# Attention scores of float32 queries and keys: one float32 matmul against three float32r passes over split operands

## What is computed

```python
q = apply_rope(rmsnorm(q, q_norm_w), rope_cos, rope_sin)
k = apply_rope(rmsnorm(k, k_norm_w), rope_cos, rope_sin)
scores = jnp.einsum('bhtd,bhsd->bhts', q, k) * scale
scores = LOGIT_SOFTCAP * jnp.tanh(scores / LOGIT_SOFTCAP)
scores = jnp.where(mask[None, None], -jnp.inf, scores)
attn = jax.nn.softmax(scores, axis=-1)
out = jnp.einsum('bhts,bhsd->bhtd', attn, v)
```

## Time and profile before

| | |
|---|---|
| median of 3 executions | 1161.46 us |
| lowest to highest | 1160.77 to 1165.43 us |
| the profiled execution | 1160.57 us |
| its span, first to last instruction | 1158.8 us |
| PE busy | 1036.8 us, 89% |
| DVE / ACT / POOL busy | 613.2 / 493.5 / 416.7 us |
| mean granted PE clock | 0.977 of full speed |

### The profile page before, as it was taken

How to read it: one execution, slowest core, us unless ns; L and a number is a source line. 1 busy time by engine, 2 the same in 40 slices (tenths; PEclk the granted TensorE clock), 3 DMA queues, 4 the chain that set the end, 5 groups by cost and what they waited for, 6 DMA issues and landing times.

```text
span 1158.8 us, 18069 instructions
## 1 busy us (share of the span) xinstructions
PE 1036.8 (89%) x5813; PEld 859.1 (74%) x5813; DVE 613.2 (53%) x1429; ACT 493.5 (43%) x905; POOL 416.7 (36%) x601
## 2 busy tenths in 40 slices
PE   4999999999999999999999999996879887777774
PEld 4689898899989889988888899895545554444443
DVE  3674546566586567578565856853374211111116
ACT  1355555455545455554544565454220222333320
POOL 2232224432225643222763322374026143444440
PEclk9999999999999999999999999998899999999995
DMA  9960000001001100100110000002010598889866
GB/s 364 340 210 0 0 0 1 1 1 38 1 1 53 71 18 1 37 1 1 68 43 8 19 19 1 1 19 83 10 55 5 134 233 211 224 224 234 227 131 217
DMA packets 59189, 95.74 MB, mean 83 GB/s; under 512 B 8203, under 2 KB 41750, under 8 KB 58608
## 3 DMA queue, kind: packets, MB, share of 16 engines
q1 hardware_dynamic: 46880, 80.66, 21.7%
q0 software_dynamic: 12240, 14.16, 6.4%
HBM read 62.17 MB, written 42.15 MB: 90 GB/s over the span
## 4 chain that ended last, share of the span: by engine, by line
PE 72%; DMA 12%; DVE 9%; issue 3%; POOL 1%; ACT 1%; SPq 0%; DVEq 0%; POOLq 0%; ACTq 0%
PE ps L1145 21%; PE ps L1168 11%; PE ps L1192 11%; DMA wds<-in_wd 9%; PE ps L1181 9%; PE ps L1357 4%; PE ps L1229 3%; PE ps L1372 3%; PE ps L1154 2%; PE ps L1175 2%; PE ps L1157 2%; DVE arena L866 2%; PE ps L1304 2%; DMA acc<-wos,arena 1%; PE ps L1126 1%
## 5 line engine op out<-in xcount | busy, mean ns | idle before, releaser
L392 POOL TENSOR_TENSOR holdp<-neghalf 128x1 f32<-128x1 f32 x139 | 30.1, 216 | 508.7 <-DVE ss L760 267.8
L541 ACT ACTIVATE prob<-ps,rn 128x512 f32<-128x512 f32 (+3 forms) x256 | 121.1, 526 | 178.4 <-PE ps L1168 178.3
L1145 PE MATMUL ps<-wh,hth 128*128 128x384 f32 x512 | 177.8, 347 | 8.5 <-DVE wl L714 4.6
L760 DVE TENSOR_REDUCE ss<-arena 128x8 f32<-128x1024 f32 x64 | 78.1, 1220 | 198.4 <-ACT arena L525 198.3
L1145 PE MATMUL ps<-wh,htl 128*128 128x384 f32 x512 | 172.4, 337 | 0.0
L1145 PE MATMUL ps<-wl,hth 128*128 128x384 f32 x512 | 172.3, 337 | 0.0
L1168 PE MATMUL ps<-qt,kt 128*128 128x512 f32 (+3 forms) x512 | 149.6, 435 | 11.6 <-DVE arena L779 5.8
L525 ACT ACTIVATE arena<-ps 128x1024 f32<-128x1024 f32 x64 | 65.6, 1025 | 221.4 <-PE ps L1145 221.4
L1192 PEld LDWEIGHTS ps<-vx,prob 128*128 128x128 f32 x1280 | 152.9, 191 | 4.0 <-POOL prob L439 0.8
L1192 PE MATMUL ps<-vx,prob 128*128 128x129 f32 (+1 forms) x1280 | 153.4, 274 | 0.5 <-POOL prob L439 0.5
L504 POOL DMA_INDIRECT acc<-wos,arena x64 | 90.2, 1409 | 142.4 <-ACT wos L649 105.0
(11 more groups left out here) (165 smaller groups left out, 1605.1 us busy)
## 6 DMA issues: line engine op xcount, KB each, us to landing
wgus<-in_wgu SPq DMA_DIRECT2D x64, 352.0 KB
wds<-in_wd SPq DMA_DIRECT2D x64, 176.0 KB
slot_rows<-pay SPq DMA_DIRECT2D x1, 7728.0 KB, 35.5
arena<-slot_rows SPq DMA_DIRECT2D x64, 120.8 KB, 3.3
warena<-in_wqkv SPq DMA_DIRECT2D x1, 4992.0 KB, 20.2
acc<-zrow SPq DMA_DIRECT2D x2, 2048.0 KB, 30.1
warena<-acc SPq DMA_DIRECT2D x8, 512.0 KB, 7.5
wos<-in_wo SPq DMA_DIRECT2D x1, 2048.0 KB, 28.3
```

The source lines that it names most:

```text
L541: act_(prob[:, OFF[j]:OFF[j] + w], sflat[:, OFF[j]:OFF[j] + w], ACT.Tanh, scale=rn[:, bass.ds(head(n), 1), TT + j:TT + j + 1].squeeze(1)). ...
L760: nc.vector.tensor_reduce(ss[:].rearrange("p (c i) -> p i c", c=2), sq, X, ALU.add).then_inc(s["ss_rdy"], 1)
L1145: last = mm(ps[:, i, 0:3 * DH], hp[:, k, i * P:(i + 1) * P], wp[:, k, :], start=(k == 0 and m == 0), stop=(k == KC - 1 and m == 2))
```

## The change

The transposed queries and keys are kept as a high part rounded to float32r and a low part, what is left. ACT writes the high parts (`qth`, and `kth` with `g` as the scale), DVE the low parts by a subtraction of the high part from the PSUM value (`qtl`), and for the keys by a multiply and subtraction in one instruction (`ktl`). Each matmul of the scores becomes three float32r matmuls into the same PSUM columns: high by high, high key by low query, low key by high query. In ACT's list the two new instructions stand between `out_t` and `exps`. DVE's two instructions now wait for ACT in place of PE. The experts' `xgt` and `gact` move to the storage of `h2s`.

```diff
-        qt = sb("qt", [P, T])
-        kt = sb("kt", [P, T])
+        qth = sb("qth", [P, T], F32R)
+        qtl = sb("qtl", [P, T], F32R)
+        kth = sb("kth", [P, T], F32R)
+        ktl = sb("ktl", [P, T], F32R)
...
-        xgt = qt[:, 0:2 * KC * C].rearrange("p (u k c) -> p u k c", u=2, k=KC)
-        gact = kt[0:C, 0:2 * M].rearrange("p (u m) -> p u m", u=2)
+        xgt = h2s.rearrange("p k t -> p (k t)")[:, 0:2 * KC * C].rearrange("p (u k c) -> p u k c", u=2, k=KC)
+        gact = h2s.rearrange("p k t -> p (k t)")[0:C, 2 * KC * C:2 * KC * C + 2 * M].rearrange("p (u m) -> p u m", u=2)
...
+            def qk_high(b, n):
+
+                if some(cnt(b, n - 1)):
+                    a.wait_ge(s["s_rdy"], 3 * cnt(b, n - 1))
+                a.wait_ge(s["qt_ps"], cnt(b, n))
+                act_(qth[:], ps[:, 2, :], ACT.Copy).then_inc(s["qth_rdy"], 1)
+                a.wait_ge(s["kt_ps"], cnt(b, n))
+                act_(kth[:], ps[:, 3, :], ACT.Copy, scale=g[:, bass.ds(head(n), 1)]).then_inc(s["kth_rdy"], 1)
...
                 cap(b, p)
                 if some(cnt(b, p - 1)):
                     out_t(b, p - 1)
+                if not (is_last(b) and static and p == H - 1):
+                    qk_high(b, p + 1)
                 exps(b, p)
...
             weights_high(0, 1)
+            a.wait_ge(s["g_rdy"], 4)
+            qk_high(0, 0)
             take(0, 1)
...
             def qk_t(b, n):
-                v.wait_ge(s["qt_ps"], cnt(b, n))
-                cp(qt[:], ps[:, 2, :]).then_inc(s["qt_rdy"], 1)
-                v.wait_ge(s["kt_ps"], cnt(b, n))
-                ts(kt[:], ps[:, 3, :], g[:, bass.ds(head(n), 1)], None, ALU.mult).then_inc(s["kt_rdy"], 1)
+                v.wait_ge(s["qth_rdy"], cnt(b, n))
+                tt(qtl[:], ps[:, 2, :], qth[:].bitcast(F32), ALU.subtract).then_inc(s["qt_rdy"], 1)
+                v.wait_ge(s["kth_rdy"], cnt(b, n))
+                nc.vector.scalar_tensor_tensor(out=ktl[:], in0=ps[:, 3, :], scalar=g[:, bass.ds(head(n), 1)], in1=kth[:].bitcast(F32),
+                                               op0=ALU.mult, op1=ALU.subtract).then_inc(s["kt_rdy"], 1)
...
-                    last = mm(sflat[:, OFF[j]:OFF[j] + w], kt[:, j * P:(j + 1) * P], qt[:, T - w:T], start=True, stop=True)
+                    for m, (kp, qp) in enumerate(((kth, qth), (kth, qtl), (ktl, qth))):
+                        last = mm(sflat[:, OFF[j]:OFF[j] + w], kp[:, j * P:(j + 1) * P], qp[:, T - w:T], start=(m == 0), stop=(m == 2))
                     if j != 1:
                         last.then_inc(s["s_rdy"], 1)
```

More of the change, by code:

```diff
@@ L212, in build @@
             wh_rdy wl_rdy h_full h_high stats aggr var_eps rstd_rdy xn_rdy hmod xt_ps ht_rdy h2t_out h2_out logit_ps
-            qkv_rdy squared k_copied v_copied ss_rdy r_tmp r_rdy q_scaled qt_ps kt_ps qt_rdy kt_rdy
+            qkv_rdy squared k_copied v_copied ss_rdy r_tmp r_rdy q_scaled qt_ps kt_ps qth_rdy kth_rdy qt_rdy kt_rdy
             s_rdy sum_inv probs pos_w capped expd p_rdy o_rdy den_rdy o_normed ot_ps ot_rdy y_rdy y_added h2s_rdy x2_rdy
```

## The result

The changed kernel took 1172.46 us (median of 8 runs, 1166.81 to 1177.83) beside 1165.53 us for the kernel before on the same chip (8 runs, 1160.77 to 1168.35): a ratio of 1.0063, 95% interval [1.0033, 1.0093]. It is slower, by 0.6%, where 1157.0 and a range of 1149 to 1165 had been said. Of the 15.5 us between 1157.0 and 1172.46, 4.1 are the starting point: the kernel before has a median of 1161.46 us over three executions and of 1165.53 over eight. The other 11.4 are the change: 6.9 slower in place of 4.5 faster. The profiled execution took 1172.74 us (span 1171.0, mean granted clock 0.966) beside 1160.57 (1158.8, 0.977).

What follows compares the result with a forecast made beforehand. Attention was taken as bound by PE, with DVE's list longer in a few rounds. Savings of 11.6 us less 6.5 and 0.7 gave 4.4 us less, 1157.0 us; range 1149 to 1165.

Steps and rivals of the forecast that it cites:

- A plain round of 11.33: Rounds bound by PE, scores to scores: 11.33 us in place of 11.60, 0.27 less in each of 43 rounds.
- the lower bound of the text (0.24): Saving of a PE-bound round: 0.24 us in place of 0.27 if each pass costs 0.003 more.
- The hop 0.72 late: DVE's list behind `qk_t`: 0.72 us later against the scores' start, because DVE waits for ACT's high parts.
- These seven rounds bit as said: DVE-bound rounds 1 (batches 1 to 3), 8 (three times), 12 (batches 0 to 2): nine, 0.72 us longer each, 6.5 in all.
- The start: Batch 0, rounds 0 and 1: PE waits 0.9 us more for the mask, some 0.2 comes back; 0.7 us lost.
- In a plain round nothing new waits: Plain rounds: the later low parts and mask still reach PE in time, `qt_rdy` with 0.6 us to spare.
- Rounds 2, 13 and 14: Round 2 taken as 0; rounds 13 and 14, bound by `q_scale` and `h_split`, gain nothing; batch 3 loses only round 14's own saving.
- The loop-back of PE's list (2.15 us of issue), the tail and the experts stay: PE's loop jump, the tail and the experts: no change in time, the jump's issue gap staying 2.15 us.
- Around the 2.15 us of the loop-back it stays 1.00: PE's granted clock around the loop jump: 1.00 in the earlier profile, used against a fall of the clock.
- PE's clock falls in the longer waits: Rival, chance 0.08: round 8's wait grows to 2.8 us, the clock falls in three rounds, 9 us lost, 1166.
- the forecast's own range of 2.5 to 7.8: Whole kernel: net saving of 2.5 to 7.8 us from the bounds of the terms, that is 1153 to 1159.

Runs made afterwards that it cites:

- the run with the hop alone: Against the kernel before: ACT makes the high parts, DVE waits for them, then copies float32, and the scores stay float32 matmuls; ratio 1.0124 [1.0101, 1.0147].

## Why the prediction was wrong

The mechanism of the gain and of its price was right, and the sizes nearly so:

- *A plain round of 11.33.* 11.36. The term that was mis-sized is the cost of a wide pass: 0.23 for the 0.227 of 512 columns, and 0.18 for the 0.173 that the earlier trace rows gave for 384; three passes of each are some 0.03 us. A saving of 0.235 for 0.27, just under the lower bound of the text (0.24), which had named this case: 1.5 us.
- *The hop 0.72 late.* DVE's instructions start 0.06 later than laid out, and round 8 grew by 0.91, round 12 of batch 0 by 0.74, round 1 by 0.73. These seven rounds bit as said; for rounds 12 of batches 1 and 2 the run with the hop alone shows it (0.67 and 0.68 longer). The start cost 0.58 for 0.7.
- *In a plain round nothing new waits.* Right: no wait of `qkv` for the low parts.
- *Rounds 2, 13 and 14.* Round 2 of batches 1 to 3 gained 0.2 where 0 was taken. Round 13 took 13.34 in place of 13.02 in batch 0 and 0.1 less in batches 1 and 2, round 14 stayed. Round 14 of batch 3 took 25.6 in both kernels; over all runs it scatters from 24.0 to 25.8, so its share of the saving can't be read.

The step that failed is the sentence "The loop-back of PE's list (2.15 us of issue), the tail and the experts stay", with "Around the 2.15 us of the loop-back it stays 1.00". The gap of the jump stayed, but what is behind it did not: the change moved a cut of the list into the scores of round 12 (a second gap of 1.30 and 0.72 us) and the clock fell there. Together 6.35 us. Nothing in the prediction asked what 12 more entries ahead of the loop do to PE's list, though the earlier trace rows showed that it is late behind the jump. The second cut was to be seen in the kernel before too, in its timeline of PE behind the scores of round 12 of batch 1:

```profile
385.81 0.60 PE L1175 MATMUL ps<-ident,arena 128*128 128x128 f32 x4
386.25 0.83 PE L1154 MATMUL ps<-ident,arena 128*128 128x128 f32 x4
386.92 0.60 PE L1157 MATMUL ps<-ident,arena 128*128 128x128 f32 x4
```

The second group starts 0.44 after the first, the third 0.67 after the second: 0.23 us are missing, at the end of the second group (which is 0.83 long in place of 0.60), 15 to 16 entries behind the jump's target (8 of the scores, 4 and 4 transposes).

The Trainium skill ("Runtime: NRT & Kernel Launch", Instruction fetch mechanics) says that an engine's instructions come by DMA in blocks of 16 KiB, 256 instructions, one after the other, and that a taken branch out of the blocks at hand must first fetch its target. The runs agree in what can be seen: the queue of instructions moved 0.75 MB in 46 packets, 16.3 KB each, in the changed kernel and 0.70 MB in 43 before, 40 and 38 with the loop written out; the second gap moved by exactly the entries that were added; and with the loop written out there was none, and the packets stand where the table above has them. If an entry is a weight load and a matmul, two instructions, a block would hold 128 entries, an estimate from the page's figure, and 8, 20 or 60 added entries would all keep the next cut out of the scores, as it was. The packets agree: in the changed kernel they come 18.8 us apart where the list runs straight on, and with 76 entries to a round of 11.37 us these are 126 entries.

The second part of the miss was among the rivals: *PE's clock falls in the longer waits*, with 2.8 us in round 8 as its place and 1166 as its time. The gap came out at 2.81, the clock fell in two of three rounds 9, at 1.6 us each in place of the 3 taken from the earlier trace rows, where it had been low for longer. It was given 0.08, because its rows had gaps up to 2.15 us with the clock at 1.00 behind them and then none under 11; 16 of 21 is what the runs show for gaps of 2.8. But the trace of the kernel before has such gaps behind the attention, at 866.89 (4.69 us) and in the experts (2.40 us), and the clock fell to 0.50 behind both. The second one, with the stretch behind it:

```profile
958.01 1.94 PE L1357 MATMUL ps<-wgus,qt 128*96 128x352 f32 x4 [2.40 <-DMA wds<-in_wd]
...
958.70:962.00 3.30, 3.30 (x11) 1.99 (x10) 0.60 (x2) 0.31 (x1) 0.00 (x0) 0.50 0.64 151
```

So a fall behind a gap of 2.8 us could have been read from the trace before, and its chance should have been higher. That rival and the cut together make the measured time.

Taken alone: no cut in the scores and no fall of the clock would have given 830.3 - 6.35 - 3.2 = 820.75 at the start of the last round, 2.6 us less than before, inside the forecast's own range of 2.5 to 7.8.

## What to carry to other kernels

A saving of 0.235 us in each of 43 rounds is as large as what a handful of gaps does to PE's clock (1.4 to 3.0 us each here). Before it is counted, look at each place where PE waits (the clock fell behind waits of 1.7 us and longer here), ask how long the wait will be afterwards, and take the work of the other engine out of that round first: here moving half of one VectorE task by two rounds was worth as much as the whole change (the last round starts at 812.53 in place of 819.90 in the written-out kernel before).

Where PE's list jumps back over many rounds, the number of instructions ahead of the loop is part of the timing. A slower result after an edit that adds instructions can be tested with a few matmuls in front of the list; if the time moves, it is layout.

## What the runs showed of the hardware that was not expected

- Behind a jump back PE's list is late twice: 1.65 to 2.21 us at the target, and again 0.65 to 2.41 us at the next cut if this lies four entries behind the target. 15 to 16 entries behind it only 0.23 us are left. A packet of instructions lands 1.72 to 1.88 us before PE goes on in the first case and 1.24 to 1.61 in the second. A jump back over one round shows no gap.
- A float32 matmul is two entries of the list, a float32r matmul one.
- Successive float32r passes over 512 columns start 0.23 us apart, over 384 columns 0.18. The first one's start is marked 0.03 us after that of the matmul before, a float32 one's 0.11, so a stretch that begins with it looks 0.08 too long.
- The granted clock fell to the 1.2 GHz level behind 16 of 21 gaps of 2.75 to 2.81 us and behind 1 of 18 of 1.73 to 1.75 us, all at the same place of the kernel, and the round behind it lost 1.4 to 3.0 us.
- A float32 matmul of 4 columns is not cheap: 30 of them took 12.96 us at the start of the kernel, 0.43 each. The clock record says 1.00 there, but in the same run passes of 384 columns start 0.32 us apart at 28 us in place of the later 0.17, so PE seems to run at half speed in the start whatever the record says.
